# Graph attention in two halves: weighing source rows half a batch at a time, weighing the batch after a four-sum batch between its additions, and placing the query products one block later

## The chip, the cores and the metric

The kernel runs on 1 core of one Trainium2 chip. The metric is the device time of the core in microseconds; the figure compared is the median over runs. One further execution was recorded by the hardware profiler, and all rows below come from it.

## The reference, cut to what matters

The program is a two-layer graph network on 2,500 nodes and 42,500 edges. The change touches only the graph attention and linear attention of the second layer, which for each edge computes:

```python
h = jnp.einsum('ni,hio->nho', x, W)                 # 8 heads x 64
e = s_src[src] + s_tgt[tgt]                         # 8 scores per edge
e = jnp.where(e >= 0, e, NEG_SLOPE * e)
m = jax.ops.segment_max(e, tgt, num_segments=n)
ex = jnp.exp(e - m[tgt])
denom = jax.ops.segment_sum(ex, tgt, num_segments=n)
alpha = ex / (denom[tgt] + 1e-16)
msgs = h[src] * alpha[:, :, None]
out = jax.ops.segment_sum(msgs, tgt, num_segments=n)
...
q = jax.nn.elu(q) + 1.0                             # linear attention beside it
k = jax.nn.elu(k) + 1.0
context = jnp.einsum('bhnd,bhne->bhde', k, v)
```

Layer 0 (relational convolution, attention, mixture of experts) stands before it, and a dense expert layer after it; neither is changed.

## The kernel before, in words

`attend` is one block in which the five engines run hand-written queues against each other, joined by semaphores. The edges, sorted by target, lie in 352 slots of 128 (a slot is one edge per partition), grouped in 88 batches of 4 slots (`BATCH`, `NBATCH`). A batch passes through these steps.

- GpSimd (`gather(s)`, L2271) issues four indirect DMAs, which fetch for 512 edges the 520 numbers of their source node (512 features, 8 source scores) into one of `RING = 6` slots of `rows`. The slot is free when TensorE has finished batch s - 6 (`agg_done`).
- SyncE (L2305) loads the target positions (`where`), `NR = 5` batches deep; VectorE makes them a one-hot matrix (`turned_hot`, L2351). TensorE (`spread`, L2569) multiplies it by the target scores, four batches ahead of use.
- VectorE takes that product (`take_n`, L2367) and forms the scores (`scores`, L2377 to L2379). ScalarE takes exponentials (`exponents`, L2486 and L2487), the second copy into `p_e`, a single PSUM buffer, which it may overwrite only when VectorE has weighed the batch before (`msg_ready`).
- VectorE multiplies the 4 x 512 features by the exponentials (`weigh`, L2385): one instruction for the batch, which releases TensorE with one increment of `msg_ready`.
- TensorE (L2634) multiplies, for each slot, a one-hot matrix of targets (made by ScalarE, L2466 and L2471) by the weighted rows, 128x260 twice; each call shows as two matmul records. The result goes to one of `NS = 2` PSUM buffers, `p_ag`.
- VectorE adds a finished sum into `acc` (`add_sum`, L2361), at the target tile's address, which it loads first (`tile_of`, L2354). Sum k may only start in PSUM when sum k - 2 is added (`agg_added`).

How many slots share one sum is fixed in `WIDTH`: most batches hold one sum of four slots. Batches 4, 12, 20, ..., 76 (ten of them) have width 1, four separate sums; this text calls them singles. Batches 8, 16, ..., 72 (nine) have two sums of two slots; it calls them pairs. So there are 127 sums. In a single, TensorE starts slot 1 only when the sum of the batch before is added, slot 2 only when its own first sum is added, and so on.

VectorE's order in iteration s is: `scores(s+1)`, `take_n(s+2)`, the additions held over, `turned_hot(s+5)`, `weigh(s)`, loads of tile numbers, and then in a pair one addition, in a single three (the last sum of the batch before and the single's first two). The single's third sum is added in iteration s+1, before `turned_hot` and `weigh(s+1)`.

Between slots, TensorE also does parts of the linear attention (`between`): of every 8 batches, key/value products (`kv_half`, L2584) lie after slots 0 and 1 of the batches with s % 8 = 0 and 2, query products (`q_part`, L2593) after slots 0 and 1 of those with s % 8 = 4, and context products (`context_part`, L2604) after slots 0 and 1 of those with s % 8 = 6. The batches with s % 8 = 4 are the singles; those with s % 8 = 0 are the pairs. ScalarE and VectorE finish the features one and two batches later (`behind`: `key_features` L2390, `query_features` L2396, `context_sum` L2402).

Of the kernel before, what the change touches and what calls it, by code (L numbers as in the profile page):

```python
# [8 lines left out]
ALU = mybir.AluOpType  # L9
# [4 lines left out]
P = 128  # L14
N = 2500
T = -(-N // P)
# [13 lines left out]
H = 8  # L30
# [3 lines left out]
BATCH = 4  # L34
# [9 lines left out]
WIDTH = [(SUP if NARROW_AT.index(s) % 2 else 1) if s in NARROW_AT else BATCH for s in range(NBATCH)]  # L44
# [1728 lines left out]
HID1 = 64  # L1773
HF = H * HID1
# [401 lines left out]
def attend(nc, io, st):  # L2176

    RING = 6
# [4 lines left out]
    HALF = ROW1 // 2  # L2183
    NC = 2 * H
    EX = BATCH * NC
    UNIT = [sum(BATCH // w for w in WIDTH[:s]) for s in range(NBATCH + 1)]
    UNIT_COLUMN = [FIRST_COLUMN[s] + j for s in range(NBATCH) for j in range(0, BATCH, WIDTH[s])]
    NUNIT = UNIT[NBATCH]
    SPAN = 8
    KV_AT, Q_AT, CONTEXT_AT = (0, 2), 4, 6  # L2190
# [3 lines left out]
    with ExitStack() as ctx:  # L2194
        sb, ps, sem = tensors(nc, ctx)
        rows = sb("rows_g", [P, RING, BATCH, ROW1])
# [19 lines left out]
        p_e = ps("p_e", [P, 512])  # L2216
# [26 lines left out]
        msg_ready = sem("msg_ready")  # L2243
# [65 lines left out]
        def _(dve):  # L2309
# [9 lines left out]
            with dve.If(wide > 0):  # L2319
                dve.sem_inc(z_added, 2)  # L2320
                one_hot_z(0, 0)
                with dve.Fori(0, NZ // UN) as i:
                    for c in range(UN):
                        s = i * UN + c
# [28 lines left out]
            def tile_of(k):  # L2353
                return dve.value_load(st.tile_of[0:1, k:k + 1], min_val=0, max_val=T - 1)  # L2354
# [8 lines left out]
            def take_n(s):  # L2363
                dve.wait_ge(n_ready, s + 1)
                if s >= NN:
                    dve.wait_ge(score_ready, s - NN + 1)
                dve.tensor_reduce(n_sb[:, s % NN], p_n[:, s % 2, 0:3 * EX].rearrange("p (j k c) -> p j c k", j=BATCH, k=3),  # L2367
                                  AX, ALU.add).then_inc(n_taken, 1)
# [9 lines left out]
                link(dve.scalar_tensor_tensor(out=x, in0=x, scalar=LEAK, in1=x, op0=ALU.mult, op1=ALU.max))  # L2378
                dve.tensor_tensor(x, x, n[:, :, H:], ALU.subtract).then_inc(score_ready, 1)  # L2379

            def weigh(s):
                dve.wait_ge(ex_ready, s + 1)
                feats = rows[:, s % RING, :, 0:HF].rearrange("p j (h o) -> p j h o", h=H)
                ex = p_e[:, 0:BATCH * H].rearrange("p (j h) -> p j h", j=BATCH)
                dve.tensor_tensor(feats, feats, ex.unsqueeze(3).broadcast_to([P, BATCH, H, HID1]), ALU.mult).then_inc(msg_ready, 1)  # L2385

            def key_features(t):
                dve.wait_ge(k_pos, t + 1)
# [41 lines left out]
            take_n(0)  # L2430
            scores(0)
            take_n(1)
            weigh(0)
            added, tiles = 0, []
            for s in range(NBATCH):
                if s + 1 < NBATCH:
                    scores(s + 1)
                if s + 2 < NBATCH:
                    take_n(s + 2)
                for tile in tiles:  # L2440
                    add_sum(added, tile)
                    added += 1
                if s + NR < NBATCH:
                    turned_hot(s + NR)
                if s == NBATCH - NR:
                    context_blocks()
                if s:
                    weigh(s)
                now = max(0, UNIT[s] - 1, UNIT[s + 1] - NS)
                after = UNIT[s + 1] - 1 if s + 1 < NBATCH else NUNIT  # L2450
                tiles = [tile_of(UNIT_COLUMN[k]) for k in range(added, after)]
                while added < now:
                    add_sum(added, tiles.pop(0))
                    added += 1
                behind(s)
# [6 lines left out]
        def _(act):  # L2462
# [19 lines left out]
            def exponents(s):  # L2482
                act.wait_ge(score_ready, s + 1)
                if s:
                    act.wait_ge(msg_ready, s)
                nc.scalar.activation(rows[:, s % RING, :, HF:], score[:, s % 2], ACT.Exp)  # L2486
                nc.scalar.activation(p_e[:, 0:BATCH * H].rearrange("p (j h) -> p j h", j=BATCH), score[:, s % 2],  # L2487
                                     ACT.Exp).then_inc(ex_ready, 1)
# [60 lines left out]
        @block.tensor  # L2549
        def _(pe):  # L2550
            wide = pe.value_load(st.wide_flag[0:1, 0:1], min_val=0, max_val=1)
            with pe.If(wide > 0):
                pe.sem_inc(z_done, 3)
                with pe.Fori(0, NZ // UN) as i:
                    for c in range(UN):
                        s, r = i * UN + c, c % RZ
                        pe.wait_ge(oh_z_ready, s + 1)
                        pe.wait_ge(z_gathered[r], 16 * (2 * i + c // RZ + 1))

                        pe.wait_ge(z_added, s + 1)  # L2560
                        pe.matmul(p_z[:, c % 2, 0:H], oh_z[:, c % 2], rows_z[:, r], start=True, stop=True).then_inc(z_done, 1)

            def spread(s, j):
                if j == 0:
                    pe.wait_ge(ohT_ready, s + 1)
                    pe.wait_ge(node_ready, s + 1)
                    if s >= 2:
                        pe.wait_ge(n_taken, s - 1)
                last = pe.matmul(p_n[:, s % 2, j * 3 * NC:(j + 1) * 3 * NC], ohT[:, s % NR, j],  # L2569
                                 node[:, s % NR, j // WIDTH[s]].rearrange("p k c -> p (k c)"), start=True, stop=True)  # L2570
                if j == BATCH - 1:
                    last.then_inc(n_ready, 1)

            def kv_half(t, k):
                if k == 0 and t == 0:
                    pe.wait_ge(st.w_kv_in, 32)
                if k == 0 and t % 2:
                    pe.wait_ge(k_low, t)
                    pe.wait_ge(k_pos, t)
                    pe.wait_ge(v_taken, t)  # L2580
                if k == 0 and t and t % 2 == 0:
                    pe.wait_ge(c_added, t // 2)
                at = t * D + k * P
                last = pe.matmul(p_kv[:, :], st.qT[:, at:at + P], st.w_kv1[:, k], start=k == 0, stop=k == K - 1)  # L2584
                if k == K - 1:
                    last.then_inc(kv_done, 1)

            def q_part(m, c, k):
                if c == 0 and k == 0:
                    pe.wait_ge(k_low, 2 * m + 2)  # L2590
                    pe.wait_ge(k_pos, 2 * m + 2)
                    pe.wait_ge(v_taken, 2 * m + 2)
                last = pe.matmul(p_q[:, :].rearrange("p (t c n) -> p c t n", t=2, c=2)[:, c], st.w_q1[:, k, c * P:(c + 1) * P],  # L2593
                                 q_pairs[:, m, k], start=k == 0, stop=k == K - 1)
                if c == 1 and k == K - 1:
                    last.then_inc(q_done, 1)

            def context_part(t, c):
                if t % 2 == 0 and c == 0:
                    pe.wait_ge(q_low, t // 2 + 1)  # L2600
                    pe.wait_ge(q_pos, t // 2 + 1)
                    pe.wait_ge(k_made, t + 2)
                    pe.wait_ge(v_taken, t + 2)
                last = pe.matmul(p_c[:, c], k_f[:, t % 2, c * P:(c + 1) * P], v_m[:, t % 2, c], start=t % 2 == 0 and c == 0, stop=t % 2 == 1,  # L2604
                                 skip_group_check=True)
                if t % 2 and c == 1:
                    last.then_inc(c_done, 1)

            def between(s, j):
                m, phase = divmod(s, SPAN)  # L2610
                if m >= T // 2 or j >= 2:
                    return
                if phase in KV_AT:
                    kv_half(2 * m + KV_AT.index(phase), j)
                for n in range(2):
                    if phase == Q_AT:
                        q_part(m, j, n)
                    if phase == CONTEXT_AT:
                        context_part(2 * m + j, n)

            for s in range(AHEAD):
                for j in range(BATCH):
                    spread(s, j)
            for s in range(NBATCH):
                r = s % RING
                pe.wait_ge(oh_ready, s + 1)
                pe.wait_ge(msg_ready, s + 1)
                for j in range(BATCH):
                    w = WIDTH[s]
                    k = UNIT[s] + j // w  # L2630
                    if j % w == 0 and k >= NS:
                        pe.wait_ge(agg_added, k - NS + 1)
                    for h in range(2):
                        last = pe.matmul(p_a[:, k % NS, h, 0:HALF], oh[:, r, j], rows[:, r, j, h * HALF:(h + 1) * HALF],  # L2634
                                         start=j % w == 0, stop=j % w == w - 1)
                    if j % w == w - 1:
                        last.then_inc(agg_done, 1)
                    if s + AHEAD < NBATCH:
                        spread(s + AHEAD, j)
                    between(s, j)  # L2640
# [682 lines left out]
```

## Time and profile before

| what | value |
|---|---|
| median of 3 runs | 2127.88 us (2123.68 to 2127.91) |
| span of the profiled execution | 2334.4 us, 206.5 us above the median |
| busy: TensorE, VectorE, ScalarE, GpSimd | 2035.6, 1287.5, 783.0, 1033.4 us |
| mean granted TensorE clock | 0.932 of 2.4 GHz |
| stage of this change in the profiled execution | about 1243 to 1801 us, 558 us |

The page's busy times are of one execution, and the busy time of TensorE is that of pipelined matmuls with modelled ends. Idle time of an engine is put down to the engine that ended the wait as far as the semaphores' events tell. "issue" means that no wait was seen. In the timelines each row is one or several merged instructions: start, busy time, engine, line, operation, names, shapes, count, and in brackets the idle time of the engine before it with what ended it.

### The profile page before, as it was taken

What the parts mean: (1) busy time and instruction counts of PE and PEld (TensorE: products, weight loads), DVE (VectorE), ACT (ScalarE), POOL (GpSimd) and SP (SyncE); (2) the same over time, 40 slices, a digit from 0 to 9 for tenths busy, and PEclk for the clock granted to TensorE, in tenths of its full rate; (3) what the DMA queues carried; (4) which work ended last, traced back from release to release, by engine and by line L of the source; (5) the groups of instructions that cost most, each with busy time, mean ns of one, the idle gap of its engine ahead of it and who ended that gap; (6) DMA issues with size and microseconds to landing.
All of it is one profiled execution on the core that took longest, in us unless ns stands there. A gap on an engine that the chain in (4) does not pass through costs nothing. (4 is left out here: it accounts for less than half of the span.)

```text
span 2334.4 us, 29468 instructions
## 1 busy us (share of the span) xinstructions
PE 2035.6 (87%) x8898; PEld 1313.2 (56%) x8898; DVE 1287.5 (55%) x2800; ACT 783.0 (34%) x2025; POOL 1033.4 (44%) x1084
## 2 busy tenths in 40 slices
PE   7999967888888888599785888888888989999999
PEld 3456633434444446499643566566666955565565
DVE  7696635666766665433365677777677832112121
ACT  4322222222222313243345454445442333322322
POOL 5687855666666540333266566556554410000000
PEclk9999978999999998699897899999889989999999
DMA  4158432322323321622247676667663300000000
GB/s 129 40 108 123 119 105 79 86 84 84 90 83 91 82 64 46 219 73 72 75 145 207 185 208 194 185 195 202 186 183 98 109 1 1 9 10 1 9 10 8
DMA packets 116242, 233.21 MB, mean 100 GB/s; under 512 B 26975, under 2 KB 71142, under 8 KB 113398
## 3 DMA queue, kind: packets, MB, share of 16 engines
q0 software_dynamic: 53168, 151.69, 23.5%
q1 hardware_dynamic: 62918, 79.64, 12.3%
q8 instruction: 74, 1.21, 0.2%
q14 instruction: 82, 0.67, 0.1%
HBM read 190.44 MB, written 40.67 MB: 99 GB/s over the span
## 5 line engine op out<-in xcount | busy, mean ns | idle before, releaser
L2634 PE MATMUL p_ag<-rows_g,oh_g 128*128 128x260 f32 x1408 | 394.8, 429 | 86.5 <-issue 43.7
L2271 POOL DMA_INDIRECT rows_g<-g_table,row_src x352 | 334.7, 951 | 234.7 <-issue 92.1
L948 POOL DMA_INDIRECT rows<-h_table,row_rel x352 | 337.7, 959 | 214.0 <-issue 89.4
L2634 PEld LDWEIGHTS p_ag<-rows_g,oh_g 128*128 128x128 f32 x1408 | 266.6, 207 | 182.4 <-issue 94.7
L3001 DVE SCALAR_TENSOR_TENSOR x<-p_yf,cw_f,x 128x256 f32<-128x256 f32 (+1 forms) x160 | 66.4, 477 | 281.3 <-PE p_yf L3161 281.3
L2385 DVE TENSOR_TENSOR rows_g<-rows_g,p_e 128x2048 f32<-128x2048 f32 x88 | 200.1, 2274 | 3.9 <-issue 3.9
L1280 PE MATMUL p_agg<-rows,oh 128*128 128x256 f32 x704 | 192.1, 414 | 1.9 <-issue 1.8
L402 POOL DMA_INDIRECT slot_table<-rec_f,dst_i x120 | 164.6, 1372 | 39.4 <-issue 39.4
L1073 DVE TENSOR_TENSOR fT<-a_sb,p_sel 128x512 f32<-128x512 f32 x200 | 128.5, 682 | 92.2 <-DMA xT_table<-xT 47.1
L1280 PEld LDWEIGHTS p_agg<-rows,oh 128*128 128x128 f32 x704 | 136.0, 204 | 62.1 <-issue 42.1
L3161 PE MATMUL p_yf<-f,h_f 128*128 128x256 f32 (+1 forms) x640 | 148.4, 386 | 0.8 <-ACT h_f L3053 0.8
L2361 DVE TENSOR_TENSOR acc<-acc,p_ag 128x520 f32 x127 | 87.6, 690 | 106.8 <-PE p_ag L2634 68.1
L3111 PE MATMUL p_1f<-qT,f 128*128 128x512 f32 (+1 forms) x320 | 142.5, 589 | 0.5 <-ACT qT L3029 0.5
L3132 PE MATMUL p_2f<-h_f,f 128*128 128x512 f32 (+1 forms) x320 | 140.7, 582 | 0.4 <-DVEq L2948 0.4
L3053 ACT ACTIVATE h_f<-p_2f,par_b,par_g 128x512 f32<-128x512 f32 (+1 forms) x80 | 61.4, 767 | 221.4 <-PE p_2f L3132 221.4
L3161 PEld LDWEIGHTS p_yf<-f,h_f 128*128 128x128 f32 (+1 forms) x640 | 119.6, 191 | 24.3 <-issue 6.2
L1299 PE MATMUL p_kv<-kf,v 128*33 128x512 f32 x320 | 90.7, 660 | 44.7 <-DVE kx L1032 28.2
L1331 PE MATMUL p_sel<-qT,sel 97*128 97x512 bf16 x240 | 80.6, 399 | 41.8 <-DVE fT L1073 31.2
L1341 PE MATMUL p_y<-fT,kvs 128*64 128x512 f32 x400 | 113.1, 645 | 0.5 <-DVE fT L1073 0.5
L2466 ACT ACTIVATE away_g<-iota,dloc 128x128 f32<-128x128 f32 x352 | 111.2, 387 | 0.0
L1811 POOL DMA_INDIRECT xg<-xn_table,from_tok x47 | 53.8, 1145 | 123.8 <-PE p_xg L1895 98.0
L2486 ACT ACTIVATE rows_g<-score_g 128x32 f32<-128x32 f32 x88 | 20.3, 230 | 252.3 <-DVE rows_g L2385 163.9
(517 smaller groups left out, 3542.4 us busy)
## 6 DMA issues: line engine op xcount, KB each, us to landing
h_table<-h_out SPq DMA_DIRECT2D x20, 1024.0 KB
where_g<-d_table SPq DMA_DIRECT2D x88, 128.0 KB
w<-in_L_ffn_W SPq DMA_DIRECT2D x16, 512.0 KB, 9.6
y_table<-yb_g SPq DMA_DIRECT2D x47, 128.0 KB, 1.7
rows<-h_table,row_rel POOLq DMA_INDIRECT x352
rows_g<-g_table,row_src POOLq DMA_INDIRECT x352
g_table<-row SPq DMA_DIRECT2D x20, 260.0 KB
f<-in_L_ffn_W SPq DMA_DIRECT2D x16, 256.0 KB, 7.2
```

The costliest lines, as they stand in the source:

```text
L402: pool.indirect_dma_start(st.slot_cells, bass.IndirectOffsetOnAxis(ap=dst_i[:, at:at + 1], axis=0), rec_f[:, at:at + 1], None).then_inc(sc ...
L948: pool.indirect_dma_start(rows[:, r, j], None, st.h_rows, bass.IndirectOffsetOnAxis(ap=st.row_rel[:, at:at + 1], axis=0)).then_inc(gathere ...
L1073: dve.tensor_tensor(fT[:, n % 3, i], a_sb[:, q % 2, i], p_sel[:, i], ALU.mult).then_inc(f_ready, 1)
L1280: last = pe.matmul(p_agg[:, k % 3, at:at + D], oh[:, r, j], rows[:, r, j], start=j % w == 0, stop=j % w == w - 1)
L1341: last = pe.matmul(p_y[64 * i:64 * i + 64], kvs[:, c, 64 * i:64 * i + 64], fT[:, n % 3, i], start=c == 0, stop=c == CH - 1, skip_group_che ...
L2271: pool.indirect_dma_start(rows[:, r, j], None, st.g_table, bass.IndirectOffsetOnAxis(ap=st.row_src[:, at:at + 1], axis=0)).then_inc(gather ...
L2385: dve.tensor_tensor(feats, feats, ex.unsqueeze(3).broadcast_to([P, BATCH, H, HID1]), ALU.mult).then_inc(msg_ready, 1)
L2466: last = nc.scalar.activation(away[:, s % 2, j], st.iota[:, :], ACT.Abs, bias=st.dloc[:, at:at + 1], scale=-1.0)
L2634: last = pe.matmul(p_a[:, k % NS, h, 0:HALF], oh[:, r, j], rows[:, r, j, h * HALF:(h + 1) * HALF], start=j % w == 0, stop=j % w == w - 1)
L3111: last = pe.matmul(p_1[:, s, 0:cols(n)], st.f1[:, e, k, s * P:(s + 1) * P], st.xnT[:, k, at:at + cols(n)], start=k == 0, stop=k == K - 1)
L3132: last = pe.matmul(p_2[:, s, 0:cols(n)], st.f2[:, e, k, s * P:(s + 1) * P], h1[:, n % 2, k, 0:cols(n)], start=k == 0, stop=k == K - 1)
L3161: last = pe.matmul(p_y[0:r, m % 2, j], h2[:, n % 2, s, j * P:j * P + r], st.f3[:, n % NE, s], start=s == 0, stop=s == K - 1)
```

## The change

`weigh` becomes two instructions, `weigh(s, 0)` for slots 0 and 1 and `weigh(s, 1)` for slots 2 and 3. Each increments `msg_ready`; TensorE waits for it before slot 0 and again before slot 2, and ScalarE's `exponents` for both. `weigh_both(s)` stands before `turned_hot(s+5)` instead of after it. In the iteration of a single, VectorE adds the sum of the batch before, weighs the first half of the next batch, adds the single's first sum, weighs the second half, and adds the single's second and third sums; the next iteration then weighs nothing. The query products move from after slots 0 and 1 of the single to after slots 1 and 2.

```diff
+    PART = BATCH // 2
...
-            def weigh(s):
+            def weigh(s, half):
                 dve.wait_ge(ex_ready, s + 1)
-                feats = rows[:, s % RING, :, 0:HF].rearrange("p j (h o) -> p j h o", h=H)
-                ex = p_e[:, 0:BATCH * H].rearrange("p (j h) -> p j h", j=BATCH)
-                dve.tensor_tensor(feats, feats, ex.unsqueeze(3).broadcast_to([P, BATCH, H, HID1]), ALU.mult).then_inc(msg_ready, 1)
+                part = slice(half * PART, (half + 1) * PART)
+                feats = rows[:, s % RING, part, 0:HF].rearrange("p j (h o) -> p j h o", h=H)
+                ex = p_e[:, 0:BATCH * H].rearrange("p (j h) -> p j h", j=BATCH)[:, part]
+                dve.tensor_tensor(feats, feats, ex.unsqueeze(3).broadcast_to([P, PART, H, HID1]), ALU.mult).then_inc(msg_ready, 1)
+
+            def weigh_both(s):
+                weigh(s, 0)
+                weigh(s, 1)
...
-            weigh(0)
+            weigh_both(0)
...
                 for tile in tiles:
                     add_sum(added, tile)
                     added += 1
+                if s and WIDTH[s - 1] > 1:
+                    weigh_both(s)
                 if s + NR < NBATCH:
                     turned_hot(s + NR)
                 if s == NBATCH - NR:
                     context_blocks()
-                if s:
-                    weigh(s)
                 now = max(0, UNIT[s] - 1, UNIT[s + 1] - NS)
                 after = UNIT[s + 1] - 1 if s + 1 < NBATCH else NUNIT
                 tiles = [tile_of(UNIT_COLUMN[k]) for k in range(added, after)]
+                if WIDTH[s] == 1:
+                    for half in range(2):
+                        add_sum(added, tiles.pop(0))
+                        added += 1
+                        weigh(s + 1, half)
+                    now = after
...
-                    act.wait_ge(msg_ready, s)
+                    act.wait_ge(msg_ready, 2 * s)
...
                 m, phase = divmod(s, SPAN)
-                if m >= T // 2 or j >= 2:
+                if phase == Q_AT:
+                    j -= 1
+                if m >= T // 2 or j not in (0, 1):
                     return
...
                 pe.wait_ge(oh_ready, s + 1)
-                pe.wait_ge(msg_ready, s + 1)
                 for j in range(BATCH):
                     w = WIDTH[s]
                     k = UNIT[s] + j // w
+                    if j % PART == 0:
+                        pe.wait_ge(msg_ready, 2 * s + j // PART + 1)
```

## Rows read from the trace of the kernel before

**Rows 1.** Busy time of each engine in the attention stage; x: instructions.

```profile
core 0: us, PE busy (x) PEld busy (x) DVE busy (x) ACT busy (x) POOL busy (x), PEclk, DMA share, GB/s
1243.00:1801.00 558.00, 463.44 (x1984) 340.97 (x1984) 385.83 (x700) 252.58 (x839) 325.81 (x343) 0.90 0.67 187
```

**Rows 2.** Timeline, VectorE: the weighing of batches 29 and 77, forty-eight batches apart.

```profile
1440.92 2.28 DVE L2385 TENSOR_TENSOR rows_g<-rows_g,p_e 128x2048 f32<-128x2048 f32 x1
...
1744.49 2.28 DVE L2385 TENSOR_TENSOR rows_g<-rows_g,p_e 128x2048 f32<-128x2048 f32 x1
```

**Rows 3.** Timeline, TensorE, at full clock: plain slots; slots with key/value and query products.

```profile
1706.22 1.12 PE L2634 MATMUL p_ag<-rows_g,oh_g 128*128 128x260 f32 x4
...
1707.21 1.12 PE L2634 MATMUL p_ag<-rows_g,oh_g 128*128 128x260 f32 x4
...
1283.02 1.04 PE L2634 MATMUL p_ag<-rows_g,oh_g 128*128 128x260 f32 x4
...
1284.87 1.04 PE L2634 MATMUL p_ag<-rows_g,oh_g 128*128 128x260 f32 x4
...
1651.81 1.04 PE L2634 MATMUL p_ag<-rows_g,oh_g 128*128 128x260 f32 x4
...
1653.25 1.04 PE L2634 MATMUL p_ag<-rows_g,oh_g 128*128 128x260 f32 x4
```

**Rows 4.** Timeline, VectorE, between two plain batches.

```profile
1715.82 2.27 DVE L2385 TENSOR_TENSOR rows_g<-rows_g,p_e 128x2048 f32<-128x2048 f32 x1
...
1718.82 0.69 DVE L2361 TENSOR_TENSOR acc<-acc,p_ag 128x520 f32 x1
1719.43 0.35 DVE L2351 TENSOR_SCALAR ohT_g<-where_g,iota_p 128x512 bf16<-128x512 bf16 x1
1719.69 2.28 DVE L2385 TENSOR_TENSOR rows_g<-rows_g,p_e 128x2048 f32<-128x2048 f32 x1
```

**Rows 5.** Timeline, GpSimd: gathers.

```profile
1624.43 0.94 POOL L2271 DMA_INDIRECT rows_g<-g_table,row_src  x1 [0.30 <-issue]
1625.68 0.94 POOL L2271 DMA_INDIRECT rows_g<-g_table,row_src  x1 [0.30 <-issue]
```

**Rows 6.** Timeline, TensorE: single 60 and the start of batch 61.

```profile
1630.23 0.38 PE L2634 MATMUL p_ag<-rows_g,oh_g 128*128 128x260 f32 x1
...
1631.47 1.11 PE L2593 MATMUL p_kv_g<-qT,w_q 128*128 128x256 f32 x4
1635.51 2.10 PE L2634 MATMUL p_ag<-rows_g,oh_g 128*128 128x260 f32 x4 [2.94 <-DVE acc L2361]
...
1642.34 0.19 PE L2569 MATMUL p_n<-node_g,ohT_g 128*128 128x48 bf16 x1
1644.67 0.84 PE L2634 MATMUL p_ag<-rows_g,oh_g 128*128 128x260 f32 x2 [2.15 <-issue]
```

**Rows 7.** Timeline, VectorE: the same stretch.

```profile
1628.04 2.28 DVE L2385 TENSOR_TENSOR rows_g<-rows_g,p_e 128x2048 f32<-128x2048 f32 x1
1634.76 0.70 DVE L2361 TENSOR_TENSOR acc<-acc,p_ag 128x520 f32 x1 [4.44 <-DMA rows<-h_table,row_rel]
...
1641.41 0.70 DVE L2361 TENSOR_TENSOR acc<-acc,p_ag 128x520 f32 x1 [1.80 <-PE p_ag L2634]
1642.03 0.35 DVE L2351 TENSOR_SCALAR ohT_g<-where_g,iota_p 128x512 bf16<-128x512 bf16 x1
1642.29 2.28 DVE L2385 TENSOR_TENSOR rows_g<-rows_g,p_e 128x2048 f32<-128x2048 f32 x1
1644.49 0.18 DVE L2377 TENSOR_TENSOR score_g<-rows_g,n_g 128x32 f32<-128x32 f32 x1
```

**Rows 8.** Timeline, TensorE: pair 72, slot 3, and batch 73.

```profile
1715.22 1.12 PE L2634 MATMUL p_ag<-rows_g,oh_g 128*128 128x260 f32 x4
...
1718.18 1.11 PE L2634 MATMUL p_ag<-rows_g,oh_g 128*128 128x260 f32 x4 [1.82 <-issue]
```

**Rows 9.** Timeline, ScalarE: exponentials of batch 61.

```profile
1630.97 0.24 ACT L2486 ACTIVATE rows_g<-score_g 128x32 f32<-128x32 f32 x1
```

## The prediction

> **What bounds the kernel now.** I read the page first, then the busy times of the attention stage, then the timelines of each engine there. The stage takes 558 us of the profiled 2334.4 us, and no engine fills it: VectorE is busy 385.8 us, GpSimd 325.8 us, and TensorE's granted clock averages 0.90 [rows 1]. The stage repeats every eight batches with one single and, alternating with it, one pair. From the weighing of batch 29 to that of batch 77 pass 303.57 us for 48 batches, 50.6 us for eight [rows 2].
>
> What would each engine need for eight batches if it never waited?
>
> TensorE: a plain slot comes every 0.99 us [rows 3], so 32 slots cost 31.6 us. A slot with half of the query products behind it lasts 1.85 us, which puts each half at 0.86; the key/value halves I take as the same. Two query and four key/value halves are 5.2 us; a slot with context products lasts 1.44 us, so two of these add 0.9 [rows 3]. Together 37.7 us.
>
> VectorE: a plain batch takes 3.87 us from weighing to weighing [rows 4]. Eight are 31.0. The single and the pair bring four more sums at 0.61 us (from a sum's start to the next instruction's, same rows), 2.4 us, and the feature work about 1.6 us. Together 35.0 us.
>
> GpSimd: a gather is issued every 1.25 us, busy 0.94 and 0.30 in between [rows 5]. Thirty-two are 40.0 us. That is the highest of the three, and the ring of six slots lets GpSimd run ahead, so it shows no waits caused by it on VectorE so far.
>
> So some 10 us of each 50.6 lie in waits between the engines, and they gather around the single. In single 60 TensorE does slot 0 and half the query products, then stands 2.94 us until the sum of batch 59 is added. It runs the next matmuls at the lower of its two clocks (four records last 2.10 us instead of 1.12). After slot 3 it stands another 2.15 us before batch 61 [rows 6]. VectorE in that time has weighed batch 60 by 1630.32, stands 4.44 us, adds, later stands 1.80 us for the third sum, and only then does 0.26 us of `turned_hot` and 2.20 us of weighing for batch 61 [rows 7]. Those 2.46 us are on TensorE's path; the batch takes 14.2 us (slot 0 at 1630.45 to 1644.67) where its work is 5.7. After a pair TensorE stands 1.82 us for the same reason [rows 8].
>
> **Two readings of the longest stall.** The last matmul of batch 59 is recorded as ending at 1630.61 [rows 6], but the addition that waits for it starts at 1634.76, 4.1 us later, and the profile names an unrelated DMA as its releaser [rows 7]. Either the signal was that late on every execution (late reading), or only when profiled (prompt reading). Outside the profile the kernel takes 2127.88 us, 206 us less than the profiled 2334.4. That loss has to sit somewhere, and a phase in which TensorE issues many small instructions and others wait on its signals is a natural place. I take prompt signals as likelier for the timed runs. The Trainium skill (Perfetto Trace Analysis, Per-instruction lifecycle) says that TensorE's end times are computed from the size of the instruction and not observed; the row agrees that end and signal can lie 4.1 us apart, but that rule does not say which of the readings holds without the profiler.
>
> **The change, part by part.**
>
> *Halves.* It removes 88 instructions of 2048 elements per partition and adds 176 of 1024. The full one lasts 2.27 us, a sum of 520 elements 0.69 us [rows 4]: 1.04 ns per element and 0.15 us fixed, so a half lasts 1.21 us. The next instruction starts 0.08 us before the full one ends (1642.29 + 2.28 against 1644.49) [rows 7]. With that overlap two halves occupy 2.26 us against 2.20, 0.06 us more per batch, 5 us in all; without any, 0.22 us and 19 us. I take the lower end since the halves follow each other on satisfied waits, but keep both. VectorE's 35.0 us per eight becomes 35.5 (36.8 at worst), still under TensorE's 37.7 and GpSimd's 40.0, so it costs nothing while those two cover it. The Trainium skill (VectorE: DVE Perf Modes, The TRN2 errata) speaks against splitting: small instructions each pay a fixed latency. By its formula, (N + 151) / 0.96 ns, two halves cost an estimated 0.16 us per batch more, 14 us if all were exposed; the trace's 0.15 us intercept agrees with it.
>
> *Earlier start.* TensorE may start slot 0 about 1.1 us earlier after a weighing and needs the second half only 1.97 us after that, when it is done. Weighing ahead of `turned_hot` gives 0.26 us more. `turned_hot(s+5)` is needed by TensorE's batch s + 1 and SyncE's load by five batches later; moved 2.3 us later it still comes at the start of TensorE's batch s. Gain where TensorE waited on a weighing of a plain batch: up to 1.4 us; elsewhere none.
>
> *The single, prompt reading.* Before: the sum of 59 is added by 1631.4, while TensorE is still in the query products until about 1632.3. Slots 1 to 3 with the second query half end near 1636.2. VectorE adds the third sum at 1636.0 at the latest, then 0.26 + 2.20 us follow: batch 61 at 1638.6. So TensorE stands 2.4 us, and a stand of 2.15 us is followed in the trace by slow matmuls (0.84 us for two records) [rows 6]; at the lower clock over one recorded stretch I price that at 1.7 us. After: VectorE adds the sum of 59 by 1631.4, weighs half of 61 by 1632.6, adds the first sum by 1633.2, weighs the rest by 1634.4 and adds the second by 1635.0. TensorE runs slot 1 from 1631.4, query products, slot 2 at 1633.3, query products, slot 3 at 1635.2, and batch 61 at 1636.2 without a wait. The exponentials that the first half needs can start once batch 60 is weighed, 1630.1; before they ran at 1630.97 [rows 9], soon enough. Gain 2.4 + 1.7 = 4.1 us. Moving the query products out of slot 0's gap removes nothing by itself: it lets slot 1 stand where the sum is ready and puts TensorE work where the two new half weighings delay the additions.
>
> *The pair, prompt reading.* TensorE reaches batch 73 about 0.65 us before the full weighing is done; the first half alone is done in time. Gain 0.65 us.
>
> So eight batches need 42.4 us before (37.7 + 4.1 + 0.65) and 37.7 after for TensorE. **What is late next** is GpSimd at 40.0 us. If its pace of 1.25 us holds without the profiler, the gain is 2.4 us per eight, 24 us over the ten; if it does not bind, 4.75 us, 47 us. No row tells which, and I take the middle, 35 us.
>
> **The sum.** 2127.9 - 35 = 2093 us. In the profiled execution, where signals are late whichever reading holds for the timed runs, I expect more, as the first rival works out: about 2334 - 91 = 2243 us.
>
> **The rivals.**
>
> *Signals are late in timed runs too.* For it: the 2.94 and 4.44 us stalls are measured. Against: 206 us vanish without the profiler. Then the single gains more: TensorE stands idle after slot 0 instead of working, its signal comes, and batch 60 takes about 7.0 us instead of 14.2. Batch 61 runs at full clock (3.95 instead of 5.63) and the pair gains 1.4. That is 10.3 us per eight, to 40.3, just above the gathers' 40.0; with some friction 41.5, so 9.1 us times ten: 2037 us.
>
> *Nothing to be measured.* The gathers already pace the timed runs, and TensorE's stands only use up their slack. For it: 40.0 us per eight is only 2.4 below my estimate of 42.4. Against: in the trace VectorE hardly ever waits for a gather. 2124 to 2130 us.
>
> *VectorE becomes the bound, slower.* It happens if timed TensorE work per batch falls below VectorE's 3.87 us and the stands around the singles were covered. Each batch then pays the split, 0.06 to 0.22 us, over 88 batches 5 to 19 us, at the `weigh` line: 2133 to 2147 us. It decides once VectorE's eight batches exceed the others' 40.0, that is at 5.0 us more than counted. Against: VectorE stands 4.44 and 1.80 us in one single [rows 7]. The skill's formula above gives 2142 us here.
>
> **Chances.** Forecast 0.64, late signals 0.15, nothing 0.13, VectorE the bound 0.08. A measurement of this kernel tells about 0.2%, 4.3 us, from no change. "Nothing" is split: 0.03 of it ends faster by more than that. Faster 0.82, same 0.11, slower 0.07. The range leaves out the slower case, the upper third of "nothing" and part of the late-signals case below 2040: 2040 to 2126. The forecast's own range is 2081 to 2104.
>
> **What the profile after would show.** 176 weighings of some 1.21 us. In a single, half weighings between the additions and no stand of TensorE before the next batch; the 2.15 us one gone, the 2.94 us one shorter. Eight batches at 40 to 42 us instead of 50.6, the granted clock of the stage above 0.90, and GpSimd's gathers nearly without gaps beyond 0.30 us. I am wrong if the second addition in a single is what TensorE now waits for, held up by the half weighing ahead of it, or if the weighing waits for ScalarE.

## The result, and the profile after

The changed kernel takes 2111.3 us (median of 5 runs, 2107.01 to 2114.33) against 2127.06 for the one before (5 runs, 2123.68 to 2127.91): a ratio of 0.9927, interval 0.9914 to 0.9940, 15.8 us or 0.7% faster. The forecast was 35 us. Its direction and its wide range (2040 to 2126) held; its size, and the forecast's own range of 2081 to 2104, did not.

The profiled execution of the changed kernel has a span of 2112.3 us. That of the kernel before had 2334.4 us; a second profile of the same kernel, taken among the experiments, has 2120.1 us. The rows ahead of the prediction therefore come from an execution that ran 206 us long, and the fair comparison is with the second profile. First the busy times of a window of 445 us, which covers the attention stage of the changed kernel and all but the last 12 us of that of the kernel before (columns as in [rows 1]: length, busy time and count of TensorE matmul, weight load, VectorE, ScalarE, GpSimd, then granted clock, DMA share, GB/s). Of the changed kernel:

```profile
1130.00:1575.00 445.00, 415.85 (x1984) 312.00 (x1985) 392.75 (x800) 257.04 (x853) 330.33 (x348) 0.98 0.82 237
```

and of the kernel before, second profile:

```profile
1130.00:1575.00 445.00, 408.06 (x1929) 308.33 (x1930) 375.34 (x692) 251.87 (x835) 327.41 (x344) 0.98 0.82 235
```

Where [rows 1] showed a clock of 0.90 and a DMA share of 0.67, both kernels really stand at 0.98 and 0.82. The distance between the weighings of batches 29 and 77, which was 303.57 us in [rows 2], reads in the second profile of the kernel before (timeline, VectorE)

```profile
1291.03 2.28 DVE L2385 TENSOR_TENSOR rows_g<-rows_g,p_e 128x2048 f32<-128x2048 f32 x1
...
1540.45 2.28 DVE L2385 TENSOR_TENSOR rows_g<-rows_g,p_e 128x2048 f32<-128x2048 f32 x1
```

and in the changed kernel

```profile
1283.59 1.21 DVE L2387 TENSOR_TENSOR rows_g<-rows_g,p_e 128x1024 f32<-128x1024 f32 x1
...
1525.11 1.22 DVE L2387 TENSOR_TENSOR rows_g<-rows_g,p_e 128x1024 f32<-128x1024 f32 x1
```

That is 249.42 against 241.52 us for 48 batches, 41.6 against 40.25 us for eight. From the first weighing to that of the last batch pass 452.3 against 438.8 us: 13.5 us, nearly the whole difference of the medians. (The two profiled spans differ by 7.8 us only, since this execution of the changed kernel came to its first weighing at 1134.2 us and that of the kernel before at 1128.8, in code that is the same in both.) What holds the changed kernel at 40.25? Its gathers (timeline, GpSimd), the first of batch 13 and the first of batch 77:

```profile
1190.21 0.95 POOL L2272 DMA_INDIRECT rows_g<-g_table,row_src  x1 [0.30 <-issue]
...
1511.35 0.94 POOL L2272 DMA_INDIRECT rows_g<-g_table,row_src  x1 [0.30 <-issue]
```

256 gathers in 321.14 us, 1.254 each, 40.1 for eight batches, as in [rows 5] with hardly a gap more. The groups by line for the stage say the same: idle time before gathers in the second profile of the kernel before, where GpSimd still waited 14.0 us for TensorE,

```profile
L2271 POOL DMA_INDIRECT rows_g<-g_table,row_src x343 | 326.7, 953 | 114.8 <-issue 100.8 <-PE p_ag L2634 14.0
```

and in the changed kernel

```profile
L2272 POOL DMA_INDIRECT rows_g<-g_table,row_src x344 | 326.7, 950 | 104.8 <-issue 103.0 <-PE p_ag L2649 1.8
```

Who waits for these gathers? VectorE, in front of the first instruction of `scores(s)`, which needs all four gathers of batch s. Its idle time there (waits of VectorE in the stage: us in total, times, longest), in the second profile of the kernel before:

```profile
DVE score_g L2377 <- DMA rows_g<-g_table,row_src: 2.3, 2, 1.2
```

and in the changed kernel:

```profile
DVE score_g L2378 <- issue: 30.0, 36, 3.3
```

The profile names no releaser for the second, but the landings fit: the last gather of batch 61 is recorded as landed at 1439.82, and `scores(61)` starts at 1439.90 after a stand of 0.81 us. In the kernel before it starts 8.9 us after that gather was issued, in the changed kernel 5.1 us after.

Now the single, where the prediction worked. Kernel before, second profile, VectorE and then TensorE around single 60 (the rows that answer to [rows 7] and [rows 6]):

```profile
1447.78 2.28 DVE L2385 TENSOR_TENSOR rows_g<-rows_g,p_e 128x2048 f32<-128x2048 f32 x1
1450.67 0.69 DVE L2361 TENSOR_TENSOR acc<-acc,p_ag 128x520 f32 x1 [0.61 <-PE p_ag L2634]
...
1456.23 2.28 DVE L2385 TENSOR_TENSOR rows_g<-rows_g,p_e 128x2048 f32<-128x2048 f32 x1
```

```profile
1455.08 1.12 PE L2634 MATMUL p_ag<-rows_g,oh_g 128*128 128x260 f32 x4
1456.04 0.19 PE L2569 MATMUL p_n<-node_g,ohT_g 128*128 128x48 bf16 x1
1458.61 1.11 PE L2634 MATMUL p_ag<-rows_g,oh_g 128*128 128x260 f32 x4 [2.39 <-DVE rows_g L2385]
```

The 4.44 us stand of VectorE is 0.61 here and the 2.94 us one of TensorE is gone. What stays is 2.39 us before batch 61; the prompt reading had 2.4. Changed kernel, the same place, VectorE and TensorE:

```profile
1441.33 2.34 DVE L2387 TENSOR_TENSOR rows_g<-rows_g,p_e 128x1024 f32<-128x1024 f32 x2
1443.60 0.35 DVE L2352 TENSOR_SCALAR ohT_g<-where_g,iota_p 128x512 bf16<-128x512 bf16 x1
1443.86 0.69 DVE L2362 TENSOR_TENSOR acc<-acc,p_ag 128x520 f32 x1
1444.46 1.21 DVE L2387 TENSOR_TENSOR rows_g<-rows_g,p_e 128x1024 f32<-128x1024 f32 x1
1445.60 0.69 DVE L2362 TENSOR_TENSOR acc<-acc,p_ag 128x520 f32 x1
1446.20 1.21 DVE L2387 TENSOR_TENSOR rows_g<-rows_g,p_e 128x1024 f32<-128x1024 f32 x1
```

```profile
1441.72 0.19 PE L2581 MATMUL p_n<-node_g,ohT_g 128*128 128x48 bf16 x1
1442.65 1.11 PE L2649 MATMUL p_ag<-rows_g,oh_g 128*128 128x260 f32 x4 [0.75 <-issue]
...
1444.60 1.14 PE L2649 MATMUL p_ag<-rows_g,oh_g 128*128 128x260 f32 x4 [0.81 <-DVE acc L2362]
...
1448.41 1.04 PE L2649 MATMUL p_ag<-rows_g,oh_g 128*128 128x260 f32 x4
1449.29 0.19 PE L2581 MATMUL p_n<-node_g,ohT_g 128*128 128x48 bf16 x1
1449.31 1.12 PE L2649 MATMUL p_ag<-rows_g,oh_g 128*128 128x260 f32 x4
```

The half weighings lie between the additions, and batch 61 follows the single at once (1449.31). But TensorE now stands 0.75 us before slot 0, until batch 60's first half is weighed, and 0.81 before slot 1: the stands moved to places where VectorE is late because it waited for gathers. The mean distance from a single's start to the next batch's fell from 8.26 to 6.29 us over the ten singles; yet eight batches fell by 1.3 us only.

### The profile page after: what moved, and what is told of

It is laid out like the page before. It is cut to its first block and busy times, and to the rows that moved or that the text cites. A ratio compares the mean times of both kernels' runs of the same rounds, so it can differ in the third digit from the quotient of the medians.

```text
span 2112.3 us, 29575 instructions
## 1 busy us (share of the span) xinstructions
PE 1955.7 (93%) x8898; PEld 1271.8 (60%) x8898; DVE 1288.4 (61%) x2888; ACT 783.5 (37%) x2025; POOL 1040.6 (49%) x1084
## 3 DMA queue, kind: packets, MB, share of 16 engines
q8 instruction: 74, 1.21, 0.2%
## 5 line engine op out<-in xcount | busy, mean ns | idle before, releaser
L948 POOL DMA_INDIRECT rows<-h_table,row_rel x352 | 343.4, 976 | 117.0 <-issue 101.4
L2649 PE MATMUL p_ag<-rows_g,oh_g 128*128 128x260 f32 x1408 | 358.5, 400 | 23.8 <-DVE rows_g L2387 10.8
L2649 PEld LDWEIGHTS p_ag<-rows_g,oh_g 128*128 128x128 f32 x1408 | 246.8, 191 | 103.5 <-issue 48.8
L2387 DVE TENSOR_TENSOR rows_g<-rows_g,p_e 128x1024 f32<-128x1024 f32 x176 | 207.2, 1214 | 0.4 <-ACT p_e L2499 0.4
L1280 PE MATMUL p_agg<-rows,oh 128*128 128x256 f32 x704 | 178.6, 392 | 0.0
L1280 PEld LDWEIGHTS p_agg<-rows,oh 128*128 128x128 f32 x704 | 127.1, 191 | 52.3 <-issue 34.6
L3126 PEld LDWEIGHTS p_1f<-qT,f 128*128 128x128 f32 x320 | 61.7, 193 | 75.3 <-issue 74.4
L1299 PE MATMUL p_kv<-kf,v 128*33 128x512 f32 x320 | 83.8, 627 | 21.9 <-DVE kx L1032 18.7
L3147 PEld LDWEIGHTS p_2f<-h_f,f 128*128 128x128 f32 x320 | 61.3, 192 | 59.0 <-issue 56.6
```

The source lines that it names most:

```text
L948: pool.indirect_dma_start(rows[:, r, j], None, st.h_rows, bass.IndirectOffsetOnAxis(ap=st.row_rel[:, at:at + 1], axis=0)).then_inc(gathere ...
L1280: last = pe.matmul(p_agg[:, k % 3, at:at + D], oh[:, r, j], rows[:, r, j], start=j % w == 0, stop=j % w == w - 1)
L3126: last = pe.matmul(p_1[:, s, 0:cols(n)], st.f1[:, e, k, s * P:(s + 1) * P], st.xnT[:, k, at:at + cols(n)], start=k == 0, stop=k == K - 1)
L3147: last = pe.matmul(p_2[:, s, 0:cols(n)], st.f2[:, e, k, s * P:(s + 1) * P], h1[:, n % 2, k, 0:cols(n)], start=k == 0, stop=k == K - 1)
```

## The experiments

**Is the long profile the kernel's own?** The kernel before, unchanged, one more profile.

> The kernel before, unchanged, profiled once more. If the late signals belonged to that one profiled execution, the span comes out within 5 us of 2126, eight batches of the stage take 41 to 42 us instead of 50.6, and TensorE stands before the batch after a single for about 2 us. If they belong to the kernel before whenever it is profiled, the span is again above 2300 us and eight batches take about 50 us.

Span 2120.1 us, 41.6 us for eight batches, rows above. The late signals belonged to that one execution. Only half of its excess lies in this stage: its first weighing came 112 us later than in the second profile, and from there to the last weighing it took 101 us more.

**Each part alone.** Three kernels: halves alone,

```diff
-            def weigh(s):
+            def weigh(s, half):
...
                 if s:
-                    weigh(s)
+                    weigh_both(s)
...
-                pe.wait_ge(msg_ready, s + 1)
+                    if j % PART == 0:
+                        pe.wait_ge(msg_ready, 2 * s + j // PART + 1)
```

the change without the move of the query products, and that move alone (on the kernel before):

```diff
-                if m >= T // 2 or j >= 2:
+                if phase == Q_AT:
+                    j -= 1
+                if m >= T // 2 or j not in (0, 1):
                     return
```

> Halves alone: weigh in two instructions with TensorE waiting for each, everything else as before (after turned_hot, no weighing between additions, query products in place). Theory G (gathers pace the stage at 40.1 us per eight batches, so only about 1.6 us per eight was to be had): the half start shortens the stand after a single by about 1.1 us, and most of the gain is there: 2114 to 2120 us. Theory I (what counts is the weighing between the additions): 2125 to 2129 us.

> The change without moving the query products. Theory G: the gathers set the pace, so it is as the changed kernel, 2108 to 2115 us. Rival Q (the query products after slot 0 delay the single once VectorE weighs between the additions): 2118 us or more.

> Only the query products one block later, the rest as before. Theory G: nothing of its own, 2125 to 2129 us. Rival Q: half of the change's gain or more, 2119 us or less.

Medians (before: 2125.3 us): halves 2111.25, ratio 0.9936 (0.9913 to 0.9960); without the move 2111.16, 0.9933 (0.9910 to 0.9956); the move alone 2110.0, 0.9931 (0.9907 to 0.9955). The first came out 3 us faster than expected. The third was a miss: I expected nothing of it, and it gives as much as the whole change. Three gains that do not add up suggest a cap, but the three do not reach it alike. VectorE's waits in front of `scores` between 1150 and 1570 us are 30.0 us in the changed kernel, 27.6 without the move, 5.1 with halves alone and 0.9 with the move alone. So the first two wait for gathers, halves alone does so in a few places (3.3 of its 5.1 us in one of them), and the move alone hardly at all: there TensorE still stands after the single, only less (timeline, TensorE, batch 61):

```profile
1447.98 0.19 PE L2569 MATMUL p_n<-node_g,ohT_g 128*128 128x48 bf16 x1
1449.84 1.11 PE L2636 MATMUL p_ag<-rows_g,oh_g 128*128 128x260 f32 x4 [1.67 <-issue]
```

Why does the move shorten the stand, from 2.42 to 1.61 us in the mean of ten? With it, half of the query products runs between slot 2 and slot 3 of the single. From slot 2's start to slot 3's now pass 1.85 us instead of 0.91, so VectorE adds the third sum and begins to weigh batch 61 earlier, counted from the end of the single.

**Take the cap away.** From batch 6 on, the fourth slot of each batch is not gathered but loaded as the first 128 table rows by a plain DMA on SyncE's queue. The bytes and all other work stay; the messages of that slot are those of wrong source nodes, and the rows are read from the same place each time.

```diff
-                for j in range(BATCH):
+                for j in range(BATCH if s < RING else BATCH - 1):
...
+            def plain(u):
+                if RING <= u < NBATCH:
+                    sp.wait_ge(agg_done, UNIT[u - RING + 1])
+                    sp.dma_start(rows[:, u % RING, BATCH - 1], st.g_table[0:P, :]).then_inc(plain_in[u % RING], 16)
```

> The kernel before with GpSimd relieved: from batch 6 on, the fourth slot of each batch is not gathered; a plain DMA on SyncE's queue loads the first 128 rows of the table in its place, so that slot's messages are those of wrong source nodes, with the same bytes and the same work on every other engine. GpSimd then needs 30 us per eight batches. Theory G (before, TensorE and VectorE set 41.6 us per eight, the gathers none of it): little changes, 2115 to 2126 us. Rival: if something else of the gathers (their landing, the ring) set the time before, it falls below 2110 us.

> The changed kernel with the same relief (fourth slot loaded from the first 128 rows by a plain DMA, so its messages are of wrong source nodes). Theory G (the gathers' 40.1 us per eight are what the changed kernel waits for, TensorE would need 37.7): eight batches take 37.7 to 38.5 us, 2078 to 2092 us, 30 us or more below the relieved kernel before. Rival V (VectorE or the signals between engines limit the changed kernel at 40 us): 2105 to 2112 us.

> Halves alone, with the same relief (fourth slot of wrong source nodes). Theory G: the parts, which gave the same time while the gathers set the pace, now come apart; halves shorten the stand after a single by about 1.1 us and that after a pair or a key/value batch by 0.3 to 0.6, so 15 to 22 us below the relieved kernel before. Rival V: no difference from the relieved changed kernel.

> Query products one block later alone, with the same relief (fourth slot of wrong source nodes). Theory G: slot 2's sum is ready before the second half of the query products instead of after, so the stand after a single shortens by 0.86 us; 8 to 12 us below the relieved kernel before, less than halves alone. Rival V: no difference from the relieved changed kernel.

| relieved kernel | median us | below relieved before | eight batches, us |
|---|---|---|---|
| before | 2122.4 | | 42.2 (span 2127.2) |
| query move alone | 2110.5 | 11.9 | 40.5 |
| halves alone | 2104.8 | 17.6 | 40.0 |
| whole change | 2088.3 | 34.1 | 38.4 |

The last column is from one profiled execution each; that of the kernel before ran about 7 us longer than its median. The kernel before hardly gains (ratio to the real one 0.9985, 0.9969 to 1.0001), so gathers did not hold it. The changed one gains 23 us, from 2111.3 to 2088.3 (ratio to the real kernel before 0.9819, 0.9804 to 0.9835). Halves alone gain 6.5 us (2111.25 to 2104.8). The query move alone gains nothing (2110.0 and 2110.5): it was not held by the cap, and what it is worth by itself only happens to end near it. So with the relief the parts come apart, because the cap had cut the whole change and trimmed the halves. In the relieved changed kernel GpSimd waits for TensorE, which is the right way round (groups by line, stage):

```profile
L2273 POOL DMA_INDIRECT rows_g<-g_table,row_src x258 | 246.6, 956 | 154.5 <-PE p_ag L2660 99.9 <-issue 54.6
```

**Do order and halves matter below the cap?** Two more relieved kernels: one without the query move, one with the new order but whole weighings.

> The changed kernel without moving the query products, with the fourth slot loaded from the first 128 rows by a plain DMA (messages of wrong source nodes). Theory G: weighing between the additions removes the stand after a single by itself; the query products in slot 0's gap cost little; 2086 to 2094 us, within 5 us of the relieved changed kernel's 2088. Rival Q (the move is needed once GpSimd no longer hides it): 2096 us or more.

> The relieved changed kernel (fourth slot of wrong source nodes) with each batch weighed by one whole instruction: earlier than turned_hot, between the first two additions of a single, query products moved, but no halves. Theory G: in a single the first sum's addition then comes 1.1 us later and holds up slot 2, and after pairs TensorE waits for the whole weighing again; 5 to 15 us above the relieved changed kernel's 2088, so 2093 to 2103 us. Rival (the halves are worth nothing, their extra instructions cost VectorE 5 us): 2083 to 2090 us.

2091.3 us without the move (3.0 above the relieved change, whose runs overlap with these: 2088.1 to 2097.7 against 2086.6 to 2091.2, so hardly told apart), 2102.2 with whole weighings (14.0 above). Below the cap the halves earn their extra instructions; whether they do in the real changed kernel, where gathers set the pace, was not run. The move, worth 12 us alone, adds about 3 once VectorE weighs between the additions.

**Make the gathers slower.** The counter-test adds work to GpSimd, first a memset of 8 numbers per batch. It also answers what the relief leaves open, whether its plain loads gain by reading the same rows each time: in it every slot gets its own rows.

```diff
                 if s >= RING:
                     pool.wait_ge(agg_done, UNIT[s - RING + 1])
+                    pool.memset(idle[:, s * 8:(s + 1) * 8], 0.0)
```

> The changed kernel with one more GpSimd instruction ahead of the gathers of each batch from batch 6 on (a memset of 8 unused numbers per partition), and nothing else. It lengthens GpSimd's five microseconds per batch by a cost c that the trace will show, perhaps 0.1 to 0.4 us. Theory G (the changed kernel waits for the gathers in every batch): the whole of it is paid, 82 c more than the changed kernel's 2111 us; with c = 0.2 that is 16 us. Rival (the gathers have slack): below 5 us more.

> The kernel before with the same extra GpSimd instruction per batch. Theory G: GpSimd has 41.6 - 40.1 = 1.5 us per eight batches, 0.19 us per batch, to spare, so only what c exceeds that is paid: with c = 0.2 about 1 us more than before's 2126, and the two kernels come within 3 us of each other or meet. Rival: it is paid in full here too, or the distance of 15 us between the kernels stays.

2108.9 and 2123.9 us, neither slower than the kernel without it. This was inconclusive: in the trace the memset fits into the 0.30 us between two gathers, and the gathers keep their pace to 0.02 us per batch. So a larger one, of 512 numbers:

```diff
+                    if s > RING:
+                        pool.wait_ge(idled, s - RING)
+                    pool.memset(idle[:, :], 0.0).then_inc(idled, 1)
```

> The changed kernel with a larger memset on GpSimd per batch from batch 6 on (512 unused numbers per partition, where the memset of 8 vanished in the 0.30 us between two gathers and cost about 0.02 us). Its cost c per batch, perhaps 0.3 to 0.6 us, is read as the growth of the distance between the gathers of successive batches. Theory G: all of it is paid, 82 c above the changed kernel: with c = 0.4, 33 us, 2143 us. Rival (slack on GpSimd): under 10 us.

> The kernel before with the same memset. Theory G: only c less 0.19 us per batch is paid: with c = 0.4, 17 us, and the two kernels end within 5 us of each other, since the gathers pace both. Rival: the 15 us between the kernels stay.

Changed kernel with it, timeline of GpSimd:

```profile
1305.53 0.54 POOL L2274 MEMSET idle_g<- 128x512 f32 x1
1306.24 0.95 POOL L2277 DMA_INDIRECT rows_g<-g_table,row_src  x1 [0.16 <-POOL idle_g L2274]
...
1310.94 0.54 POOL L2274 MEMSET idle_g<- 128x512 f32 x1
1311.65 0.95 POOL L2277 DMA_INDIRECT rows_g<-g_table,row_src  x1 [0.16 <-POOL idle_g L2274]
```

A batch of gathers now takes 5.41 us here and 5.45 on average, instead of 5.02, so its cost c is 0.43 per batch, over 82 batches. Paid in full that is 35 us; the changed kernel went from 2111.3 to 2144.4, 33 us. The kernel before had 0.19 us per batch to spare (a batch took 5.20, its gathers 5.01), should pay (0.43 - 0.19) x 82 = 20 us and went from 2125.4 to 2142.0, 17 us. The two kernels, 15 us apart, are now 2.4 us apart; their gathers keep the same pace, 5.45 and 5.44 us per batch. No version tried that computes the whole output is faster than the changed kernel by more than the runs can tell.

## Why the prediction was right or wrong

**Right.** The prompt reading of the signals; the stand after the single (2.4 us forecast, 2.42 mean of ten in the second profile) and its removal (0 after); the stand after a pair (0.65 forecast, 0.55, now 0); a half weighing of 1.21 us (1.214); two halves in 2.26 us (the first starts at 1441.33, `turned_hot` at 1443.60, 2.27); the name and the pace of what is late next, GpSimd at 40.0 us for eight batches (40.1). The formula of the Trainium skill (VectorE: DVE Perf Modes, The TRN2 errata), an estimated 1.224 us for a half, agrees with the measured 1.214. By that estimate two halves cost 0.16 us more than the whole; the trace shows 2.27 against 2.20 us, 0.07 more.

**The step that failed** is the end of the working: "No row tells which, and I take the middle, 35 us." Rows 5 did tell. A pace of 1.25 us per gather was in hand, nothing in the trace made it a product of the profiler, and the second profile, 214 us shorter, shows it unchanged; the relief and the counter-test show that it binds the changed kernel. A floor that is reached caps a gain; it is not one end of a mean. With the cap taken at its word the forecast was 24 us, "2.4 us per eight". That is still more than 15.8, and the rest lies in the next term.

**The second term, mis-sized,** is the 1.7 us per single for the lower clock. It was read off a row of the long execution [rows 6], where TensorE had also stood 2.94 us in the same single. Even there it was not the rule: batches 21 and 53 ran at full speed after stands of 2.47 and 2.39 us, eight of ten did not. In the second profile a stand of about 2.4 us is followed by full-speed matmuls after seven of the ten singles (batch 61: four records in 1.11 us); only batches 5, 21 and 69 take 5.6 us for 3.95 us of work, partly or wholly at the lower clock. That is 0.5 us per single on average, and eight batches before took 41.6 us, not 42.4. 41.6 less 40.1 is 1.5 us for eight batches, which is of the size of the measured 15.8 over 88. The share is not fixed: in the relieved kernel before, six of ten batches after a single were slow, and the timed runs of the kernel before lie between 2119.9 us at a granted clock of 0.968 and 2135.0 at 0.961. The changed kernel's profile has no slow batch after a single.

**A smaller step that failed** is the sentence that moving the query products "removes nothing by itself". Alone it took 0.8 us from the stand after each single and left one slow batch behind the singles instead of three, and the kernel went from 2125.3 to 2110.0 us. The working had the products in the wrong place: what counts is not slot 0's gap, from which they went, but the time behind slot 2, where they arrived.

**The relieved pair** gives 34.1 us where the forecast had 47 for a kernel without the cap, from 42.2 to 38.4 instead of from 42.4 to 37.7. On the side before, the lower clock cost less than priced. On the side after, 0.7 us for eight batches stay above TensorE's bare work. Half of them lie in the pair (s % 8 = 0), which takes 6.05 us where the priced work is 5.68; the rest is in the single and in the plain batches with s % 8 = 5 and 7. The other plain batches take the priced 3.95 us.

**The profiled execution** was forecast at 2243 us, on the ground that signals are late whenever the kernel is profiled. It took 2112.3: the lateness did not come back in any later profile.

**The rivals.** Late signals in timed runs: refuted by the second profile. "Nothing" had the right mechanism, gathers that pace the stage, but put it into the kernel before; the relieved kernel before shows that it was not paced by them. VectorE as the bound: refuted, the relieved change has VectorE doing the same work at 38.4 us for eight.

## What to carry to other kernels

Work out the bare time of every engine for one period before pricing any stall. The highest of them caps every gain, and if a row gives its pace, use the cap and do not average it with the gain without it. When several edits each give the same gain and do not add up, look for the engine that none of them touches, and then check by its waits which of the edits really reach it: one of the three here did not. If a profiled execution runs far longer than the timed ones, take its durations and its pace but not its stalls; a clock penalty read from it is a stall too.

## What the runs showed of the hardware

- A profiled execution ran 206 us (9.7%) longer than the timed ones, with the durations of VectorE's and GpSimd's instructions as usual (2.28 us for a weighing, 0.94 for a gather). In this stage the excess sat in waits for TensorE's signals (4.1 us after the recorded end of a matmul) and in matmuls at the lower clock behind them; another profile of the same kernel had a wait of 0.61 us in that place. What delays the signals was not found.
- The same stand of TensorE, about 2.4 us, was followed by a batch at the lower clock in three of ten cases in one profile (granted clock 0.72 from 1166 to 1172 us, behind the first single, against 1.00 from 1458 to 1463) and in six of ten in another, the relieved kernel before. After stands of 1.3 us (halves alone) it was none of ten.
- The median distance of indirect gathers of 128 rows on GpSimd's queue, 1.25 us, was the same within 0.01 us in every profile, with or without the other engines' stands. A memset of 0.12 us between two of them cost 0.02 us, one of 0.54 us cost 0.43, so that about 0.1 us of either was hidden in the 0.30 us gap. What fills the gap was not shown.
